# Folded keys' DRAM copy of a decoder layer: pair of heads laid out outside the batch, stores in rows of 4928 bytes, loads in two transfers

## The reference

```python
x = x + attn(layernorm(x), W_q, W_k, W_v, W_o)                 # 16 heads of 16
x = x + xattn(layernorm(x), ctx, mask, W_Q, W_K, W_V, W_O)     # 16 heads of 64, 77 keys
x = x + ffn(layernorm(x), W_fc, b_fc, A_fc, B_fc, W_proj, b_proj, A_proj, B_proj)
```

## Time and profile before

| | us |
|---|---|
| median of 3 runs | 632.96 (631.59 to 637.38) |
| profiled execution, its time | 640.39 |
| its span, first to last instruction | 638.6 |
| mean granted TensorE clock of the span | 0.942 |

### The profile page before, as it was taken

The page is one execution under the profiler, slowest core; times in us unless marked ns, Lnnn a source line. Parts: engine busy times, 40 slices in busy tenths (PEclk is TensorE's granted clock), DMA queues, the critical chain, the costliest instruction groups (busy, mean ns, idle before and its releaser), DMA issues.

```text
span 638.6 us, 11817 instructions
## 1 busy us (share of the span) xinstructions
PE 528.9 (83%) x4334; PEld 449.0 (70%) x4334; DVE 394.3 (62%) x1093; ACT 301.3 (47%) x484; POOL 249.0 (39%) x317
## 2 busy tenths in 40 slices
PE   2488779877987889889988997899899899957955
PEld 2376666665867767878778776878887687846755
DVE  4657622488867963796388548954983683554332
ACT  2323344432362765166535654663556277426323
POOL 5820021455256355155252526272465016522210
PEclk9779986987797999999999999999999999989969
DMA  5598997966040414051315232325140601111000
GB/s 186 167 233 174 193 216 143 225 218 205 26 100 1 150 34 121 1 160 52 88 49 147 61 83 72 89 60 118 37 112 19 157 22 42 37 41 38 1 16 17
DMA packets 63709, 62.45 MB, mean 98 GB/s; under 512 B 6868, under 2 KB 60804, under 8 KB 63652
## 3 DMA queue, kind: packets, MB, share of 16 engines
q1 hardware_dynamic: 62148, 56.74, 34.8%
q0 software_dynamic: 1504, 4.95, 2.2%
HBM read 38.28 MB, written 23.10 MB: 96 GB/s over the span
## 4 chain that ended last, share of the span: by engine, by line
PE 54%; DVE 23%; ACT 8%; issue 5%; DMA 5%; POOL 3%; SPq 1%; DVEq 0%; ACTq 0%; POOLq 0%
PE banks L798 9%; PE banks L799 8%; PE banks L800 8%; PE banks L958 5%; DVE banks L2382 4%; PE banks L1049 4%; PE banks L1060 4%; PE banks L935 4%; PE banks L1122 2%; DMA x_in<-in_x 2%; PE banks L972 2%; ACT probs L1752 2%; DMA fold_raw<-fold_dram 2%; DVE hid_lo L2337 2%; PE banks L832 1%
## 5 line engine op out<-in xcount | busy, mean ns | idle before, releaser
L2382 DVE CUSTOM_DVE_ANT_0 banks<-banks,causal_qk 128x256 f32<-128x256 f32 (+1 forms) x256 | 84.1, 388 | 13.0 <-PE banks L935 11.2
L582 POOL TENSOR_SCALAR_AFFINE_SELECT probs<-probs 128x256 f32<-128x256 f32 x128 | 52.2, 435 | 70.1 <-ACT probs L1752 70.1
L565 POOL TENSOR_TENSOR work<-work,rc 128x616 f32<-128x616 f32 x32 | 40.5, 1266 | 99.7 <-DVE rc L2482 99.7
L1752 ACT ACTIVATE probs<-banks 128x768 f32<-128x768 f32 x64 | 51.7, 808 | 32.5 <-PE banks L958 31.8
L1720 ACT ACTIVATE work<-banks 77x512 f32<-77x512 f32 (+1 forms) x72 | 43.2, 600 | 48.4 <-PE banks L1049 44.0
L572 POOL TENSOR_TENSOR fold_lo<-fold_raw,fold_hi 128x616 fp32r<-128x616 f32 x32 | 48.6, 1523 | 43.4 <-ACT fold_hi L1720 43.4
L2480 DVE TENSOR_REDUCE sm<-work 128x8 f32<-128x616 f32 x32 | 25.4, 793 | 51.0 <-ACT work L1782 50.9
L935 PE MATMUL banks<-k_stack,q_stack 96*128 96x256 f32 (+1 forms) x256 | 42.0, 288 | 13.0 <-DVE mneg L2382 9.7
L958 PE MATMUL banks<-q_stack,k_stack 100*128 100x128 f32 (+1 forms) x256 | 47.1, 309 | 5.7 <-DMA q_stack<-mnegT 2.7
L935 PEld LDWEIGHTS banks<-k_stack,q_stack 96*128 96x128 f32 x256 | 36.2, 197 | 20.2 <-DVE mneg L2382 11.6
L2337 DVE TENSOR_TENSOR late<-banks,late 128x512 fp32r<-128x512 f32 x40 | 27.4, 684 | 35.0 <-ACT late L1720 35.0
(11 more groups left out here) (190 smaller groups left out, 1574.7 us busy)
## 6 DMA issues: line engine op xcount, KB each, us to landing
fold_raw<-fold_dram SPq DMA_DIRECT2D x32, 308.0 KB, 3.1
fold_dram<-work SPq DMA_DIRECT2D x8, 616.0 KB, 8.5
rot_dram<-rot_s_hi SPq DMA_DIRECT2D x16, 256.0 KB, 3.0
rot_dram<-rot_s_lo SPq DMA_DIRECT2D x16, 256.0 KB, 2.8
q_stack<-rot_dram SPq DMA_DIRECT2D x32, 128.0 KB, 2.7
k_stack<-rot_dram SPq DMA_DIRECT2D x32, 128.0 KB, 3.0
fold_dram<-fold_raw SPq DMA_DIRECT2D x4, 616.0 KB, 6.1
fold_dram<-fold_raw_hi SPq DMA_DIRECT2D x4, 616.0 KB, 8.4
```

The lines of the kernel that those rows point to most:

```text
L582: last = pool.affine_select(out=diagonal, in_=diagonal, compare_op=ALU.is_ge, fill=0.0, base=0, pattern=[[0, 2], [1, P]], channel_multipli ...
L1752: act.activation(probs[:, n:n + 2, :], bank[:, 0:2, P:4 * P], ACT.Exp, scale=SCALE).then_inc(p_ok, 1)
L2382: last = dve.tensor_tensor_reduce(out=held[:, at], in0=held[:, at], in1=bias, scale=-1.0, scalar=HUGE, op0=ALU.add, op1=ALU.min, accum_out ...
```

## The change

`fold_dram` is laid out as [group, k, 128, pair within the group, sequence, 154]. A store of one m and one k now writes, for each partition, 4928 bytes that are contiguous in DRAM too. A load of (b, g) finds rows of 616 bytes instead of 1232, since the two pairs of a group lie 4928 bytes apart, and is issued as two DMAs, one for each k, of 154 KB in 256 rows each. ScalarE waits for both. The orders of all engines are the same.

```diff
-        fold_dram = nc.dram_tensor("fold_dram", [NB, H // GH, KD, P, GW], F32, kind="Internal").ap()
+        fold_dram = nc.dram_tensor("fold_dram", [H // GH, KD, P, 2, NB, 2 * S2], F32, kind="Internal").ap()
@@ store_fold
                 for k in range(KD):
-                    sp.dma_start(fold_dram[:, g, k, :, c * 2 * S2:(c + 1) * 2 * S2].rearrange("b p n -> p b n"),
+                    sp.dma_start(fold_dram[g, k, :, c],
                                  stage[m % 2][k].rearrange("p b a s -> p b (a s)")).then_inc(fold_st[m % 2], 16)
@@ load_fold
-                sp.dma_start(raws["fold"][:].rearrange("p (k g n) -> p k g n", k=KD, n=GW)[:, :, g % 2],
-                             fold_dram[b, g].rearrange("k p n -> p k n")).then_inc(g_ld[g], 16)
+                to = raws["fold"][:].rearrange("p (k g c n) -> p k g c n", k=KD, g=2, c=2)[:, :, g % 2]
+                for k in range(KD):
+                    sp.dma_start(to[:, k], fold_dram[g, k, :, :, b]).then_inc(g_ld[g], 16)
@@ fold_hi (ScalarE)
-                act.wait_ge(g_ld[g], 16 * (b + 1))
+                act.wait_ge(g_ld[g], 16 * KD * (b + 1))
```

## The result

The changed kernel is slower: 640.1 us median (636.9 to 648.26, 13 runs) against 632.96 of the kernel before, measured again beside it (631.59 to 638.38, 13 runs). The ratio is 1.0072, with a 95% interval of 1.0043 to 1.0102. That is 4.6 us by the ratio and 7.1 by the medians. I had said 627, with 620 to 635 as the range.

What follows compares the result with a forecast made beforehand. It took TensorE's gap at 87.5 us, behind short-row stores, and the low clock after it as what to remove: 640.39 - 2.7 - 5.0 + 1.6 = 634.3 profiled, 626.9 on the median's scale; predicted 627, range 620 to 635.

Steps and rivals of the forecast that it cites:

- What bounds the kernel: Store stage: TensorE waits 2.68 us at 87.5 us for an 8 KB DMA behind stores; then 16.8 us at clock 0.51.
- the 7.7 us that I hoped to gain: Store stage: 2.7 us from closing TensorE's gap plus 5.0 us from the clock staying high.
- The prediction's last line: Most likely wrong in the clock, over half the gain, or if timed runs do not fall to the low level there.
- The stores, 2.7 + 5.0 us: Long store rows close the gap at 87.5 us (2.7) and keep the clock at 1.00 behind it (5.0).
- My estimate from the Trainium skill: Stores: about 3 cycles of overhead per packet, so they gain only 11%, a pair taking 5.0 us instead of 5.6.
- The loads, +1.6 us: Split loads: 0.4 us each, three on the chain (1.2), plus 0.4 for the x load behind one on SP.
- 0.4 us of caution: Each load: 0.4 us taken for rows half as long, though 0.4 + 2.7 = 3.1 made it no later.
- My upper bound, nine waits of 0.4: Loads: 3.6 us if all nine ScalarE waits grew by 0.4 and each were on the path.
- E: Halves of a load do not overlap; nine waits add 24.3 us: 657, or 649.4 on the median's scale; chance 0.10.
- C: Stores: bytes take the time, not rows; gap shrinks by 0.6, clock still falls: 641.4, or 634.0; chance 0.12.
- F: Store still written as 8 rows a partition, leaving only the loads' price: 642.0, or 634.5; chance 0.04.
- B: Gap closes but the clock falls anyway a few us later: 639.3, or 631.9; chance 0.18.

Runs made afterwards that it cites:

- the second profile: The kernel before, unchanged, profiled and timed once more; ratio to before 1.0001, span 630.2 us instead of 638.6.
- the split-only run: Kernel before with each load issued as two DMAs, one for each k; layout and stores as before; ratio to before 0.9982.
- the moved `shifts`: Kernel before with shifts(0, 1), two DMAs of 8 KB, issued on SP ahead of store_fold(5); ratio to before 0.9994.
- pair inside: Layout with partition outside the sequence, pair inside: stores of 616-byte rows 1232 apart, split loads of 1232-byte rows; ratio to before 0.998.
- short rows close together: Sequence outermost, stores in 616-byte rows as before, loads two DMAs of 256 rows lying 616 bytes apart; ratio to before 1.0053.
- the even padding: Changed kernel with 64 unused bytes behind each row of 4928 bytes, so rows lie 4992 apart throughout; ratio to before 1.007.
- the uneven one: Changed kernel with 64 unused bytes behind each partition's two rows of 4928 bytes; ratio to before 0.9969, once more 0.9995.
- one load of short rows: Changed kernel with partition outermost within a group and each load one DMA of 512 rows of 616 bytes; ratio to before 1.0046.
- the long stores alone: Changed kernel with the load of before, one DMA with rows of 1232 bytes, reading wrong folded keys; ratio to before 0.9942.
- the second measurement: The changed kernel itself, timed again with six runs; ratio to before 1.0107.
- the same, padded: One DMA of 512 rows of 616 bytes for each load, with 64 unused bytes behind each partition's rows; ratio to before 1.001.

## Why the prediction was wrong, point by point

**"What bounds the kernel": the reading was right, the execution was not typical.** The gap, its length, the 8 KB transfer that ended it and the clock behind it are in the rows. That the stores' short rows caused it was argued: the second profile has the same rows and the same order and no gap. The changed kernel's profile came out as forecast there, down to the start of `values2`, but so does that of the kernel before without the gap. The second profile of the same kernel has no gap, and neither have the split-only run and the moved `shifts`. The sign was in my own numbers: the profiled execution took 640.39 us where the median was 632.96. I treated the 1.2% as a scale and multiplied by 0.988. The difference of 7.4 us was nearly the 7.7 us that I hoped to gain. I took the gain off once more from a median that, as the small timed gain of the long stores suggests but doesn't show, had mostly no such gap. The prediction's last line names this as a way to be wrong, and gives it no price.

**The stores, 2.7 + 5.0 us: mis-sized.** For landing and issue times the step held (3.8 us; issues mostly 0.32 to 0.43, some up to 1.45). In timed runs the long stores are worth little. Five kernels with them and with loads that are not slow stand at 0.9942, 0.9954, 0.9969, 0.9995 and 1.001, in the mean 0.9974. Four with stores in short rows (split only, moved shift, pair inside, before again) are at 0.9982, 0.9994, 0.998 and 1.0001, mean 0.9989. The difference is 0.15%, about 1 us; with the fifth such kernel, short rows close together at 1.0053, it is 0.28%, 1.8 us. So 1 to 2 us, little more than a hint, against 7.7 in the sum. The failed step is the premise that the gap and the slow clock behind it would be there to be removed in the timed runs. That a lead passes through to the end was right where nothing else differs: the second profile of before still has 8.4 of its 8.8 us at the end.

My estimate from the Trainium skill ("DMA: Bandwidth & Descriptors", "Why small descriptors are slow") has an error of arithmetic: eight packets of 20 + 3 cycles against one of 154 + 3 are 184 against 157, 15% less and not 11%, and 4.8 us for the pair instead of 5.0. The measured landing fell by more, from 8.5 us, or 6.5 in the second profile, to 3.8.

**The loads, +1.6 us: mis-sized by three times or more.** Against the even padding, the uneven one is 5.1 us faster; against one load of short rows, the long stores alone are 5.7 us faster. The row that I used for the issue, 0.33 and 0.43 us of the stacks' loads, was of another shape: split loads with two distances do take 0.41 to 0.42, those of the changed kernel 0.59. With the landing that makes 0.59 + 2.8 = 3.4 us for the second half where I had 3.1 from the same sum. I did add 0.4 us of caution, so the landing's price for each load was about right. SP's was half of what it is: two issues of 0.59 in place of one of 0.37 hold up what stands behind them by 0.8 us, and I had 0.4.

What was wrong beside it was the count: I let the delay count three times on the chain and once on SP. The chain of one execution names only the waits that ended last there. Both profiles of before have three loads on it, the even padding has six and the one load of short rows seven. Behind 323 us, as far back as every chain can be followed, the four profiles with slow loads (the changed kernel twice and these two) have four or five loads on it and the eleven others two or three. The waits of `fold_hi` tell the same: 13.6 to 15.5 us in the four, 6.6 to 10.6 in the eleven others. From the first `fold_hi` to the last it takes 479 to 483 us in the four, 481.6 in the mean, and 474 to 482 in the eleven, 476.5 in the mean. These 5.1 us are the timed cost again, though single profiles overlap. The largest step, 1.7 us, is at `load_fold(7, 2)`, where all four wait longer (2.7 to 4.2 us) than ten of the eleven (1.9 to 2.6). My upper bound, nine waits of 0.4, would have given 3.6. What shares the longer issue and the later landing have in the 5 us isn't shown.

**Sum.** 1 to 2 us gained and 5 to 6 lost give +3 to +5 us, and the ratio says 0.72%, 4.6 us; the second measurement says 1.07%, with an interval from 0.34 to 1.8%.

**The rivals.** None had it. E, the only slower one, was about halves of a load that run one after the other; the split alone costs nothing. C is refuted by the landing of 3.8 us, F by the packets. B is refuted by the clock, in the profile. The case that came, a gain that most runs already have beside loads slower than their bytes, was not among them, and the 12% for slower had the wrong mechanism.

**The clock as noise.** Over 264 runs of all these kernels, each compared with its own kernel's mean, a mean granted clock lower by 0.01 goes with 3.1 us more (correlation -0.80). Single runs of the kernel before lie between 631 and 646 us, and much of that goes with the clock. A profiled execution is one draw of it.

**Still open.** Why loads with several DRAM rows a partition at one distance take 0.56 to 0.59 us to issue and 0.3 to 0.4 more to land isn't shown; the runs show that they do. For stores only the longer issue is shown: with one distance they land in 6.2 to 8.1 us, no later than with two. The layout with short rows close together, whose loads are not slow and which is 0.5% slower, isn't explained. Nor is it shown in how many timed runs of the kernel before the gap of 2.7 us occurs, since only their mean clock is known.

## What to carry to other kernels

If the profiled execution is slower than the median by about as much as one event in it costs, ask for that event in a second profile before you count on removing it. Price a DMA by a row of its own shape, rows and distances on both sides; where the issue comes out at 0.5 to 0.6 us with several DRAM rows for each partition, try some bytes of padding behind each partition's rows (64 here), which cost nothing that shows and gave back 5 us. And let a delay that comes 32 times count at more places than those where the old chain shows it.

## What the runs showed of the hardware

All rows are medians of a profile, ranges those of several groups or profiles; "one" distance means that it is the same from each DRAM row to the next, taken partition by partition, "two" that the step to the next partition is another.

| DMA on SP | rows | DRAM distances | issue, ns | landing, us |
|---|---|---|---|---|
| load, before | 256 of 1232 | two | 366 | 3.0 to 3.1 |
| half load, split only | 128 of 1232 | one row a partition | 410 | 2.3 |
| half load, short rows near | 256 of 616 | two | 414 | 2.5 |
| half load, changed kernel | 256 of 616 | one | 590 | 2.8 |
| half load, padded evenly | 256 of 616 | one | 590 | 2.8 |
| half load, padded | 256 of 616 | two | 418 to 424 | 2.4 to 2.5 |
| whole load, one DMA | 512 of 616 | one | 562 | 3.5 |
| the same, padded | 512 of 616 | two | 366 | 3.1 |
| store, before, two profiles | 1024 of 616 | two | 360 to 1222 | 5.6 to 8.5 |
| store, pair inside | 1024 of 616 | one | 546 to 670 | 6.2 to 8.1 |
| store, changed kernel | 128 of 4928 | one row a partition | 326 to 429 | 3.0 to 4.5 |

Halving a load's rows from 1232 to 616 bytes costs little as long as they have two distances: nothing for the whole load (3.1 us both times), 0.1 to 0.2 us for half loads (2.4 to 2.5 against 2.3). A 308 KB load in two halves of long rows is complete 0.3 to 0.4 us sooner than in one (0.4 + 2.3 against 3.0 to 3.1).
